# SyncE's queue: the address loads of all sorted blocks ahead of the ninth block's rows, the first finished batch's store five loads later

## The chip, the cores and the metric

One core of one Trainium2 chip. The time is the device time of one execution in microseconds. Three runs of the kernel before gave 222.42, 222.91 and 529.38 us, a median of 222.91 us.

## The reference

Eight sequences of 375 frames with 128 features go through three layers: a convolution bottleneck with feed-forward and a max-pool over three frames, softmax attention inside each sequence, and a mixture of eight experts of which each frame takes its best two. Cut to the expert layer, which the change touches:

```
gate_logits = relu(xf @ gw1 + gb1) @ gw2 + gb2
top_w, top_idx = top_k(softmax(gate_logits), 2);  top_w = softmax(top_w)
combine[t, top_idx] += top_w
for e in range(8):
    out += combine[:, e:e+1] * (gelu(xf @ we1[e] + be1[e]) @ we2[e] + be2[e])
return h + out
```

## The kernel before

Every engine works through a list of pieces that is written out by hand (`PE_ORDER`, `DVE_ORDER`, `ACT_ORDER`, `POOL_ORDER`, `SP_ORDER`); a piece is a name and a number, and it first waits on the semaphores of what it needs. Each list is executed strictly in order, so a piece that waits holds everything behind it on its engine.

The expert layer is done in two ways. Three of the eight sequences (0, 6, 7) are dense: TensorE computes all eight experts for them (`D1` L1182 and `D2` L1189), and VectorE adds each result with its weight (`da`, L930). These pieces are mixed into the whole second half as filler. The other five sequences are sorted: GpSimd scatters each row twice, by expert, into the scratch array `xs` in HBM (`scat`, L541; each expert has 2048 places), and the sorted rows are worked through in blocks of 128.

There are 37 blocks. Blocks 0 to 7 are the first block of each expert; their place in `xs` and their weights (already in SBUF as `w_all`) are known when the kernel is written. Blocks 8 to 36 are the further ones. Which expert each belongs to is known only when all rows are counted: VectorE writes the table `tab_x` (L951) with the first row of each. SyncE reads it one number at a time into a register:

- `rg.n` (L422): load block n's first row from `tab_x` into a register; in the trace a TENSOR_LOAD, a FUSED_REGOPS and a SEQ_ASSERT. `rg.8` to `rg.36`, 29 of them. The register is kept until block n's pieces have used it.
- `lx.n` (L436): fetch the 128 rows of block n from `xs` into one of 18 buffers `blk_x` (64.5 KB). `lx.0` waits until all 30 scatters have landed (s_scat); `lx.n` waits for `T.(n-9)` on TensorE and, from n = 18, for the scatter that used its buffer.
- `lw.n` (L444), n from 8: copy the block's expert's weights from `w_all` into one of seven buffers `blk_w` (321 KB, SBUF to SBUF), at a register offset. From n = 15 it waits for `yv.(n-7)`, the last reader of the buffer's former content.
- `od.n` (L464, L466): store a finished dense sequence; `od.0` waits for the eighth `da`. `c4` (L429) are copies for the scatters, `yl` (L453) loads of the results at the end, `out` stores of the sorted sequences.

On TensorE a block is `T.n` (L1198, transpose of `blk_x`), `L1.n` (L1205, first product) and `L2.n` (L1214, second product). VectorE or ScalarE copies after `T` (`xT`, L817, L666), ScalarE does the gelu (`gl`, L672), VectorE the bias and copy to `yblk` (`yv`, L956), and GpSimd scatters `yblk` into `ys` (`so`, L547). When all of `ys` has landed, SyncE loads it back (`yl`), VectorE combines (`fin`, L965, L971) and SyncE stores. All copies, from whichever queue, run on the core's 16 DMA engines.

A few pieces of `PE_ORDER` around the blocks that are named later: `T.8 T.9 L2.5 ... L1.8` (the first use of a `blk_w`), `... L2.11 T.15 L1.13`, `T.24 D1.32`, `L2.24 T.28`, `D1.35 T.32 T.33 L2.30`.

Of the kernel before, what the change touches and what calls it, by code (L numbers as in the profile page):

```python
# [120 lines left out]
so.27 so.28 so.29 so.30 so.31 so.32 so.33 so.34 so.35 so.36  # L121
"""
SP_ORDER = """
c4.1 c4.2 c4.3 c4.4 c4.5 rg.8 rg.9 rg.10 rg.11 rg.12 rg.13 rg.14 rg.15 od.0 rg.16 rg.17 rg.18 rg.19 rg.20 rg.21
rg.22 rg.23 rg.24 rg.25 rg.26 lx.0 lx.1 lx.2 lx.3 lx.4 lx.5 lx.6 lx.7 lx.8 lw.8 lx.9 lw.9 lx.10 lw.10 lx.11 lw.11
rg.27 lx.12 rg.28 lw.12 lx.13 lw.13 lx.14 lw.14 lx.15 rg.29 rg.30 lw.15 lx.16 lw.16 lx.17 lw.17 lx.18 lw.18 lx.19
lw.19 rg.31 lx.20 lw.20 rg.32 rg.33 lx.21 lw.21 lx.22 lw.22 lx.23 lw.23 lx.24 lw.24 rg.34 lx.25 lw.25 lx.26 lw.26
lx.27 lw.27 lx.28 lw.28 rg.35 lx.29 lw.29 lx.30 lw.30 lx.31 lw.31 lx.32 lw.32 lx.33 lw.33 lx.34 lw.34 rg.36 lx.35
lw.35 lx.36 lw.36 yl.0 yl.1 yl.2 od.1 yl.3 out.0 yl.4 out.1 out.2 out.3 od.2 out.4
"""  # L130


# [1128 lines left out]
```

How the kernel before makes its waits and increments, by code:

```python
        def wait(eng, name, value):  # L333
            if value > 0:
                eng.wait_ge(S[name], value)
# [15 lines left out]
        def wait_so(eng, n):  # L351
            if n >= 0:
                eng.wait_ge(s_so[n % YBUF], 16 * NT * (n // YBUF + 1))
# [4 lines left out]
        def weights(eng, n):  # L359
            if n < E:
                eng.wait_ge(S["be1"], 1)
                return w_all[:, n, :]
            eng.wait_ge(s_bw[(n - E) % WSLOTS], 16 * ((n - E) // WSLOTS + 1))
            return blk_w[(n - E) % WSLOTS][:]
# [17 lines left out]
        @block.sync  # L383
# [24 lines left out]
            for c in range(HC):  # L408
                sp.dma_start(w_all[:, :, H + c * D:H + (c + 1) * D],
                             we2[:, c * 128:(c + 1) * 128, :].rearrange("e p d -> p e d")).then_inc(S["wt"], 16)
            sp.dma_start(w_all[:, :, 2 * H + HC:WROW], be2.unsqueeze(0).broadcast_to([128, E, D])).then_inc(S["wt"], 16)
            sp.dma_start(be2_sb[:], be2).then_inc(S["wt"], 16)
            sp.wait_ge(S["blank"], 2)
            sp.dma_start(xs.rearrange("(q p r) d -> p q (r d)", p=128, r=RI),
                         blank[:].rearrange("p r d -> p (r d)").unsqueeze(1).broadcast_to([128, PER // RI, RI * XW]))\
# [9 lines left out]
                    wait_nth(sp, "xn4", n)  # L425
                    if k >= 2:
                        sp.wait_ge(s_copy[k % 2], 32 * (k // 2))
                    for lo, hi in SPLIT:
# [2 lines left out]
                    i = n % SLOTS  # L431
                    if n == 0:
                        sp.wait_ge(s_scat, 16 * NI * NS)
                    wait(sp, "T", n - LOADS + 1)
```

## Time and profile before

| | |
|---|---|
| Median of three runs | 222.91 us |
| The profiled execution | 221.66 us, its span 219.9 us, mean granted TensorE clock 0.993 |
| Busy in the span | PE 204.4 us (93%), PE weight loads 166.6, DVE 154.4 (70%), ACT 136.9 (62%), POOL 112.9 (51%) |
| Chain that ended last | PE 71%, DVE 8%, SyncE's queue 6%, ACT 5%, issue 4%, DMA 3% |

The span is the profiled part of the execution; the 1.76 us between it and the execution's time lie outside. A share of the chain is the time that the chain of work that ended last spent on that engine. Block numbers do not stand in the trace; they follow from the order lists by counting.

### The profile page before, as it was taken

What the parts mean: (1) busy time and instruction counts of PE and PEld (TensorE: products, weight loads), DVE (VectorE), ACT (ScalarE), POOL (GpSimd) and SP (SyncE); (2) the same over time, 40 slices, a digit from 0 to 9 for tenths busy, and PEclk for the clock granted to TensorE, in tenths of its full rate; (3) what the DMA queues carried; (4) which work ended last, traced back from release to release, by engine and by line L of the source; (5) the groups of instructions that cost most, each with busy time, mean ns of one, the idle gap of its engine ahead of it and who ended that gap; (6) DMA issues with size and microseconds to landing.
All of it is one profiled execution on the core that took longest, in us unless ns stands there. A gap on an engine that the chain in (4) does not pass through costs nothing.

```text
span 219.9 us, 5429 instructions
## 1 busy us (share of the span) xinstructions
PE 204.4 (93%) x1553; PEld 166.6 (76%) x1553; DVE 154.4 (70%) x688; ACT 136.9 (62%) x302; POOL 112.9 (51%) x168
## 2 busy tenths in 40 slices
PE   6997788999999999999999999999999989699990
PEld 5864656659857986898678967889989768599780
DVE  6379999998998998979599944484426233224895
ACT  2234997998989688776679248456655547335430
POOL 7746776611630147676774775015777766472000
PEclk9999999999999999999999999999999999999997
DMA  5999999940010012102111121587597898712773
GB/s 157 244 270 305 330 405 406 402 170 3 0 35 1 3 35 58 53 23 80 52 47 37 38 70 48 141 259 246 165 308 232 286 303 304 270 36 71 195 226 106
DMA packets 26000, 35.31 MB, mean 161 GB/s; under 512 B 4083, under 2 KB 18838, under 8 KB 25971
## 3 DMA queue, kind: packets, MB, share of 16 engines
q1 hardware_dynamic: 23137, 30.60, 43.4%
q0 software_dynamic: 2240, 4.00, 5.8%
q10 hardware_dynamic: 594, 0.36, 0.6%
q8 instruction: 13, 0.21, 0.4%
q14 instruction: 16, 0.13, 0.2%
HBM read 10.61 MB, written 14.39 MB: 114 GB/s over the span
## 4 chain that ended last, share of the span: by engine, by line
PE 71%; DVE 8%; SPq 6%; ACT 5%; issue 4%; DMA 3%; POOL 1%; DVEq 0%; ACTq 0%
PE PS L1189 11%; PE PS L1182 10%; PE PS L1124 7%; PE PS L1106 7%; PE PS L1214 5%; PE PS L1205 4%; PE PS L989 4%; PE PS L1113 4%; DMA blk_x<-xs 3%; PE PS L1001 3%; SPq L444 3%; PE PS L1101 3%; PE PS L1018 2%; SPq L436 2%; DVE acc L965 2%
## 5 line engine op out<-in xcount | busy, mean ns | idle before, releaser
L547 POOL DMA_INDIRECT ys<-yblk,blk_x x37 | 36.0, 973 | 28.1 <-DVE yblk L956 19.3
L517 POOL TENSOR_TENSOR rstd<-mv,mhalf 125x3 f32<-125x3 f32 x32 | 27.7, 867 | 41.0 <-DVE mv L698 40.7
L661 ACT ACTIVATE gd<-PS,bias 128x373 f32<-128x373 f32 x48 | 27.1, 574 | 15.4 <-PE PS L1182 10.8
L541 POOL DMA_INDIRECT xs<-rows_x,pos_x x30 | 29.9, 996 | 13.0 <-issue 8.4
L1182 PE MATMUL PS<-xt_sb,w_all 128*128 128x373 f32 x96 | 35.7, 482 | 0.0
L1189 PEld LDWEIGHTS PS<-w_all,gd 128*125 128x125 f32 x288 | 33.6, 187 | 2.1
L1189 PE MATMUL PS<-w_all,gd 128*125 128x128 f32 x288 | 34.6, 273 | 0.0
L672 ACT ACTIVATE gb_t<-PS,blk_w 128x128 f32<-128x128 f32 x58 | 18.1, 365 | 15.1 <-issue 8.8
L930 DVE SCALAR_TENSOR_TENSOR x_sb<-PS,comb,x_sb 125x128 f32<-125x128 f32 x72 | 20.7, 343 | 5.8 <-PE PS L1189 4.9
L1182 PEld LDWEIGHTS PS<-xt_sb,w_all 128*128 128x128 f32 x96 | 15.7, 190 | 5.0 <-issue 0.9
L956 DVE TENSOR_TENSOR yblk<-PS,blk_w 128x128 f32<-128x128 f32 x29 | 8.4, 290 | 15.8 <-PE PS L1214 15.5
L1106 PE MATMUL PS<-xn_t,q_t 128*125 128x373 f32 x48 | 17.8, 486 | 0.0
L1124 PE MATMUL PS<-xn,prob_t 125*125 125x129 f32 (+1 forms) x144 | 17.6, 275 | 0.0
L1214 PE MATMUL PS<-blk_w,gb_t 128*128 128x128 f32 x116 | 17.4, 277 | 0.0
L1124 PEld LDWEIGHTS PS<-xn,prob_t 125*125 125x125 f32 (+1 forms) x144 | 16.7, 187 | 0.8 <-issue 0.4
L1205 PE MATMUL PS<-xb_t,blk_w 128*128 128x128 f32 x116 | 17.2, 275 | 0.0
L817 DVE COPY xb_t<-PS 128x128 f32<-128x128 f32 x27 | 7.8, 289 | 13.2 <-PE PS L1198 10.6
L1205 PEld LDWEIGHTS PS<-xb_t,blk_w 128*128 128x128 f32 x116 | 15.5, 191 | 1.8 <-issue 0.3
L1214 PEld LDWEIGHTS PS<-blk_w,gb_t 128*128 128x128 f32 x116 | 15.0, 191 | 0.7 <-issue 0.3
L831 DVE TENSOR_REDUCE nmax<-PS 125x1 f32<-125x373 f32 x24 | 12.8, 544 | 2.6 <-PE PS L1106 1.8
L637 ACT ACTIVATE prob_t<-PS 124x373 f32<-124x373 f32 (+1 forms) x23 | 9.9, 482 | 6.0 <-PE PS L1113 5.6
L631 ACT ACTIVATE prob<-PS,nmax 125x373 f32<-125x373 f32 x24 | 12.5, 573 | 1.5 <-DVE nmax L831 1.2
(201 smaller groups left out, 409.4 us busy)
## 6 DMA issues: line engine op xcount, KB each, us to landing
blk_w<-w_all SPq DMA_DIRECT2D x29, 321.0 KB, 3.1
xs<-blank SPq DMA_DIRECT2D x1, 8256.0 KB, 25.3
blk_x<-xs SPq DMA_DIRECT2D x37, 64.5 KB, 3.0
yg<-ys SPq DMA_DIRECT2D x5, 336.0 KB
x_sb<-in_x SPq DMA_DIRECT2D x4, 336.0 KB
out<-x_sb SPq DMA_DIRECT2D x8, 168.0 KB
xt_sb<-in_xt SPq DMA_DIRECT2D x3, 375.0 KB, 5.4
w_all<-in_we SPq DMA_DIRECT2D x1, 1024.0 KB
```

The costliest lines, as they stand in the source:

```text
L517: pool.tensor_tensor(rstd[i][:, n % 2, :], mv[i][:, n % 2, :, 1], mhalf[:], ALU.pow)\
L541: pool.indirect_dma_start(xs, bass.IndirectOffsetOnAxis(ap=pos_x[:, b // 2, s, i:i + 1], axis=0), rows_x[:, k, s, j, :], None, bounds_chec ...
L547: pool.indirect_dma_start(ys, bass.IndirectOffsetOnAxis(ap=blk_x[n % SLOTS][:, t, D:XW].bitcast(u32), axis=0), yblk[n % YBUF][:, t, :], No ...
L661: act.activation(gd[:, k % GD, c, 0:TP], of("D1", n)[:, 0:TP], ACT.Gelu, bias=bias128[:, 2 + k % E * HC + c:3 + k % E * HC + c]).then_inc( ...
L672: last = act.activation(gb_t[n % 2][:, c, :], of("L1", n)[:, c * BLK:(c + 1) * BLK], ACT.Gelu, bias=w[:, 2 * H + c:2 * H + c + 1])
L930: last = dve.scalar_tensor_tensor(flat(h2[:, b, :])[j], flat(of("D2", n)[0:P, :])[j], w[:, j, b % 2, e:e + 1], flat(h2[:, b, :])[j], ALU.m ...
L1106: pe.matmul(f[0:P, 0:TP], q_t[:, s, OFF[j]:OFF[j] + P], xn_t[:, s, :], start=True, stop=True)\
L1124: last = pe.matmul(f[0:P, j * (D + 1):(j + 1) * (D + 1)], prob_t[0:ROWS[c], s, c, OFF[j]:OFF[j] + P], xn3[0:ROWS[c], s, c, :], start=(c == ...
L1182: pe.matmul(f[:, 0:TP], w_all[:, k % E, c * 128:(c + 1) * 128], x32[:, DENSE[k // E], 0:TP], start=True, stop=True).then_inc(S["D1"], 1)
L1189: last = pe.matmul(f[0:P, j * D:(j + 1) * D], gd[:, n % GD, c, OFF[j]:OFF[j] + P], w_all[:, n % E, H + c * D:H + (c + 1) * D], start=(c == ...
L1205: last = pe.matmul(f[:, c * BLK:(c + 1) * BLK], w[:, c * 128:(c + 1) * 128], xb_t[n % 2][:], start=True, stop=True)
L1214: last = pe.matmul(f[:, t * D:(t + 1) * D], gb_t[n % 2][:, c, t * 128:(t + 1) * 128], w[:, H + c * D:H + (c + 1) * D], start=(c == 0), sto ...
```

## The change

Only `SP_ORDER` differs: the same pieces, in another order.

```diff
-c4.1 c4.2 c4.3 c4.4 c4.5 rg.8 rg.9 rg.10 rg.11 rg.12 rg.13 rg.14 rg.15 od.0 rg.16 rg.17 rg.18 rg.19 rg.20 rg.21
-rg.22 rg.23 rg.24 rg.25 rg.26 lx.0 lx.1 lx.2 lx.3 lx.4 lx.5 lx.6 lx.7 lx.8 lw.8 lx.9 lw.9 lx.10 lw.10 lx.11 lw.11
-rg.27 lx.12 rg.28 lw.12 lx.13 lw.13 lx.14 lw.14 lx.15 rg.29 rg.30 lw.15 lx.16 lw.16 lx.17 lw.17 lx.18 lw.18 lx.19
-lw.19 rg.31 lx.20 lw.20 rg.32 rg.33 lx.21 lw.21 lx.22 lw.22 lx.23 lw.23 lx.24 lw.24 rg.34 lx.25 lw.25 lx.26 lw.26
-lx.27 lw.27 lx.28 lw.28 rg.35 lx.29 lw.29 lx.30 lw.30 lx.31 lw.31 lx.32 lw.32 lx.33 lw.33 lx.34 lw.34 rg.36 lx.35
-lw.35 lx.36 lw.36 yl.0 yl.1 yl.2 od.1 yl.3 out.0 yl.4 out.1 out.2 out.3 od.2 out.4
+c4.1 c4.2 c4.3 c4.4 c4.5 rg.8 rg.9 rg.10 rg.11 rg.12 rg.13 rg.14 rg.15 rg.16 rg.17 rg.18 rg.19 rg.20 od.0 rg.21
+rg.22 rg.23 rg.24 rg.25 rg.26 rg.27 rg.28 rg.29 rg.30 rg.31 lx.0 lx.1 lx.2 lx.3 lx.4 lx.5 lx.6 lx.7 rg.32 rg.33
+rg.34 rg.35 rg.36 lx.8 lw.8 lx.9 lw.9 lx.10 lw.10 lx.11 lw.11 lx.12 lw.12 lx.13 lw.13 lx.14 lw.14 lx.15 lw.15
+lx.16 lw.16 lx.17 lw.17 lx.18 lw.18 lx.19 lw.19 lx.20 lw.20 lx.21 lw.21 lx.22 lw.22 lx.23 lw.23 lx.24 lw.24
+lx.25 lw.25 lx.26 lw.26 lx.27 lw.27 lx.28 lw.28 lx.29 lw.29 lx.30 lw.30 lx.31 lw.31 lx.32 lw.32 lx.33 lw.33
+lx.34 lw.34 lx.35 lw.35 lx.36 lw.36 yl.0 yl.1 yl.2 od.1 yl.3 out.0 yl.4 out.1 out.2 out.3 od.2 out.4
```

`od.0` stands behind `rg.20` instead of `rg.15`. `rg.27` to `rg.31` stand ahead of `lx.0`; before, they were spread from `lx.12` to `lx.20`. `rg.32` to `rg.36` stand between `lx.7` and `lx.8`; before, they were spread from `lx.21` to `lx.35`. Behind `lx.8` nothing but `lx` and `lw` is left until `yl.0`.

## Rows read from the trace of the kernel before

**Rows 1.** Busy time by stretch: us from:to, PE PEld DVE ACT POOL, clock, DMA share, GB/s

```profile
156.00:188.90 32.90, 29.70 (x230) 26.43 (x228) 11.55 (x43) 18.59 (x58) 23.35 (x24) 1.00 0.84 281
175.00:180.00 5.00, 4.03 (x29) 3.28 (x28) 1.56 (x6) 2.81 (x8) 3.19 (x5) 1.00 0.94 309
...
170.00:180.00 10.00, 8.53 (x63) 7.33 (x62) 3.12 (x12) 5.34 (x17) 6.96 (x9) 1.00 0.88 293
180.00:190.00 10.00, 8.27 (x63) 7.09 (x62) 2.82 (x11) 5.37 (x16) 5.72 (x6) 1.00 0.88 301
190.00:205.00 15.00, 15.00 (x117) 13.60 (x116) 6.28 (x24) 6.11 (x16) 6.82 (x7) 1.00 0.33 101
205.00:220.00 15.00, 9.30 (x61) 7.50 (x59) 11.89 (x45) 4.01 (x7) 0.00 (x0) 0.89 0.59 169
```

**Rows 2.** TensorE in order of time, L1198: T.15, T.24, T.28, T.33 [idle before]

```profile
158.34 0.27 PE L1198 MATMUL PS<-ident,blk_x 128*128 128x128 f32 x1
...
174.18 0.33 PE L1198 MATMUL PS<-ident,blk_x 128*128 128x128 f32 x1 [0.50 <-DMA blk_x<-xs]
...
179.50 0.33 PE L1198 MATMUL PS<-ident,blk_x 128*128 128x128 f32 x1 [0.84 <-DMA blk_x<-xs]
...
188.90 0.33 PE L1198 MATMUL PS<-ident,blk_x 128*128 128x128 f32 x1 [1.73 <-DMA blk_x<-xs]
```

**Rows 3.** SyncE's queue in order of time: start, us, issue; from lx.0 on

```profile
136.75 4.27 SPq L436 DMA_DIRECT2D blk_x<-xs  x9
...
151.53 0.46 SPq L436 DMA_DIRECT2D blk_x<-xs  x1
156.00 0.51 SPq L444 DMA_DIRECT2D blk_w<-w_all  x1
...
161.46 0.50 SPq L444 DMA_DIRECT2D blk_w<-w_all  x1
162.80 0.35 SPq L436 DMA_DIRECT2D blk_x<-xs  x1
...
167.89 0.50 SPq L444 DMA_DIRECT2D blk_w<-w_all  x1
...
174.40 0.50 SPq L444 DMA_DIRECT2D blk_w<-w_all  x1
175.15 0.40 SPq L436 DMA_DIRECT2D blk_x<-xs  x1
...
177.07 0.49 SPq L444 DMA_DIRECT2D blk_w<-w_all  x1
178.62 0.34 SPq L436 DMA_DIRECT2D blk_x<-xs  x1
...
183.90 0.38 SPq L436 DMA_DIRECT2D blk_x<-xs  x1
```

**Rows 4.** The address loads, L422, of 119 to 128.1 us: min/median/max ns

```profile
L422 SPq TENSOR_LOAD <-tab_x x8: 264/266/487, 120.0 to 124.1; - x8
```

**Rows 5.** SyncE's waits over the span: total us, times, longest

```profile
SPq L464 <- DVE x_sb L930: 3.9, 2, 3.5
SPq L444 <- DVE yblk L956: 2.5, 1, 2.5
...
SPq L436 <- DMA xs<-rows_x,pos_x: 0.6, 1, 0.6
```

**Rows 6.** Block fetches L436, 141 to 191 us: issue to landing

```profile
DMA to landing us min/median/max: 2.6/3.3/4.0
```

**Rows 7.** VectorE in order of time: yv.15

```profile
165.68 0.29 DVE L956 TENSOR_TENSOR yblk<-PS,blk_w 128x128 f32<-128x128 f32 x1 [0.71 <-PE PS L1214]
```

**Rows 8.** GpSimd in order of time: the scatters so.4 and so.36

```profile
153.72 0.98 POOL L547 DMA_INDIRECT ys<-yblk,blk_x  x1 [0.30 <-DVE yblk L956]
...
198.45 0.97 POOL L547 DMA_INDIRECT ys<-yblk,blk_x  x1 [0.30 <-issue]
```

## The prediction

> **What bounds the kernel now.** I read busy time by stretch first, then TensorE in order of time, then SyncE's queue, to see who holds whom. TensorE is the engine to follow: it is busy for all 15.00 us from 190 to 205, and the end behind that is a chain on VectorE (11.89 of 15 us) that starts from TensorE's last dense products [rows 1]. In the sorted stage it is not full: from 156 to 188.9 us it works 29.70 of 32.90 us, so 3.20 us are lost, 1.47 of them from 170 to 180 and 1.73 from 180 to 190 [rows 1]. The reader is to see in rows 2 what ends these gaps: three times the transpose of a block waits for its rows, T.24 for 0.50 us, T.28 for 0.84 and T.33 for 1.73, each released by a DMA into blk_x; the rest of the 1.47 is shorter pieces of the same kind. The trace names no other cause of idle time there.
>
> Why are the rows late? Two suspects. One is SyncE's sequencer: from 156 on it hands out a fetch and a weight copy per block and hardly ever waits; its only long wait on `yv` is the 2.5 us that end at lw.15, 156.00 [rows 3, 5]. A pair without a load between takes about 1.3 us, since the gap from an issued lw to the next lx is 0.25 us (174.90 to 175.15) [rows 3]. Where a load of an address stands in the gap, it is 0.84 us (lw.19 ends at 161.96, lx.20 begins at 162.80) and 1.06 us (177.56 to 178.62) [rows 3]: a load costs SyncE 0.59 to 0.81 us, I take 0.7. The other suspect is the DMA engines: their mean share over the same 32.9 us is 0.84, over 170 to 190 it is 0.88, and the fullest five microseconds have 0.94 [rows 1]. Both are near their limit, and that decides the size of the gain.
>
> **The change part by part.** Ahead of the batch store: five loads (rg.16 to rg.20) move ahead of od.0. Eight loads began at 120.0, the last at 124.1 [rows 4], so one costs here some 0.59 us, and od.0 then waited up to 3.5 us for VectorE [rows 5]. Five loads take 2.9 us (3.5 at 0.7) and fit into this wait. od.0 keeps its time, and its own three issues are not longer. Behind od.0 stood eleven loads, and again eleven stand there (rg.21 to rg.31), so lx.0 keeps its time, 136.75; there it waited 0.6 us for the scatters [rows 5], which is a second cushion. Cost 0; without the cushion in od.0 the five would push lx.0 by 2.9 less 0.6.
>
> Ahead of lx.8: five loads (rg.32 to rg.36) now stand in front of it, uncovered on SyncE. lx.8, the last of the nine fetches that end at 141.02 [rows 3], goes 3.0 to 4.1 us later (5 x 0.59 to 5 x 0.81). Queued behind are lw.8 and all later pairs. By lx.15, today issued at 151.53, two removed loads (rg.27, rg.28) have given time back, so three are left: 1.8 to 2.4 us, issued at 153.3 to 153.9. With 3.3 us to landing (4.0 at most [rows 6]) it lands at 156.6 to 157.9, and T.15 is due at 158.34 [rows 2]: the tightest place of the front, and it holds by 0.4 us at the worst corner. lw.15 then has four removed loads against five added ones, one load late, 0.6 to 0.8 us, inside the 2.5 us that SyncE waited there for yv.8. At 156.00 the old and new queues are therefore level. Cost 0; if the cover is gone, T.14 and T.15 are late next.
>
> Behind 156.00: six loads (rg.31 to rg.36) are gone, 6 x 0.7 = 4.2 us of SyncE. What can take their place is the ring of seven weight buffers: lw.22, today 167.89, may go no sooner than yv.15, which ends at 165.97 [rows 3, 7], so at most 1.9 us sooner where three loads would give 2.1. That limit moves along when TensorE is no longer held, as `yv` follows TensorE. At lx.24 one gets some 1.6 to 2.1 us, more than T.24's 0.50; at lx.28 four loads, 2.8 us, more than the 0.84. So I count the whole 1.47 us of 170 to 180 as won.
>
> T.33 is the place that sets the size. TensorE is ready for it at 188.90 - 1.73 = 187.17 today, and at 185.70 once 1.47 are won. lx.33 has five loads ahead of it: issued at 183.90 - 3.5 = 180.4, and at today's 5.0 us from issue to use (183.90 to 188.90 [rows 2, 3]) it would be there at 185.4, in time. But those 5.0 us, against a median of 3.3 [rows 6], say that this fetch stood in a backlog. By the DMA engines: from 156 to 188.9 they did 0.84 x 32.9 = 27.6 us of full work. At 0.94 this takes 29.4 us and ends at 185.4, at 0.88 it takes 31.4 and ends at 187.4. Between the two ends I take 0.91, as the stream has no gaps left but the share of 0.88 was reached over 20 us that held three of the loads: 30.3 us, 186.3, so T.33 still waits 0.6 us. The gain is 3.20 - 0.6 = 2.6 us; the ends are 0 (share stays 0.84) and 3.20 (all idle time of TensorE).
>
> The Trainium skill ("DMA: Bandwidth & Descriptors", Rules for kernel authors) speaks against the change here: spreading DMAs over issuing engines brings no bandwidth, because all run on the same 16 engines, it only saves the sequencer's issue time. Issue time is also all that this change saves; by that rule alone the gain would be near the low end, by SyncE's rows alone the full 3.2.
>
> Behind the blocks: GpSimd scatters back to back every 1.28 us (0.98 and 0.30 idle). From so.4 at 153.72, 32 of these put so.36 at 194.7, today it is at 198.45 [rows 8], so this queue allows 3.8 us and doesn't stop 2.6. TensorE's full stretch from 190 and VectorE's tail [rows 1] shift as they are; the loads of the results wait for so.36 and shift as well.
>
> **Sum.** 0 + 0 - 2.6 on the profiled execution's 221.66 gives 219.1. The median, 222.91, is 1.25 us above that execution; on its scale it is 220.3. A measurement of this kernel can tell about 2%, 4.5 us, from no change, and the gain is below that.
>
> **The rivals.**
> The DMA engines are the bound. For it: 0.88 over 20 us, the backlog at lx.33. Against: they stood at 0.94 for five microseconds, and each removed load is a gap in the issue stream. At 0.88, T.33 waits until 187.4, 1.7 us, and the gain is 1.5: 221.4. The skill's rule above is this case.
> No gain at all: the new order's 29 addresses held at once (19 in the old) do not fit SyncE's registers and are read again at use, or the waits on TensorE come from latency and just move. For it: the trace shows 19 held, not 29. Against: exactly one TENSOR_LOAD to each of the eight [rows 4], so nothing is reread at 19. 222.9.
> Slower: the front is not covered, because loads in a burst cost more than those seen. At 1.5 us each, lx.0 is late by 5 x 1.5 - 3.5 - 0.6 = 3.4, lx.8 by 10.9, lx.15 (two loads of 0.7 given back) by 9.5; it lands at 151.53 + 9.5 + 3.3 = 164.3, T.15 waits 6.0, less the 3.2 behind: 2.8 slower, 225.7. It decides from 1.2 us a load on (lx.15 late by 6.5, T.15 by 3.0, about even). Against: eight in a row took 0.59 each [rows 4], the dearest here 0.81.
>
> **How the numbers follow.** The forecast 0.58, gain 2.0 to 3.2, its own range 219.7 to 220.9. The DMA engines as the bound 0.20. No gain 0.11. The slower case 0.05. Faster by more than 4.5 us 0.06: only if SyncE's lead brings more than TensorE's idle time, or through scatter of runs. The range is 218.8 to 222.7: down by all 3.20 us and, for scatter, somewhat more than the 0.5 us between the two ordinary runs; up to nearly no change, which leaves out the slower case, half of no gain and the far gains. Slower by over 2% is half of the slower case and a little scatter, 0.03; faster 0.06; within, 0.91.
>
> **What would show it.** Right: od.0 still near 128.1 and lx.0 near 136.75; lx.8 three to four us later; lw.15 still released by yv.8 near 156.0, its wait shorter than 2.5; no address load behind lx.8; lx.33 3 us or more sooner; T.24 and T.28 without a wait and T.33 with under 1 us; the DMA share above 0.88 from 160 to 185; the last `yv` 2.6 us sooner. Wrong: TensorE waits at T.8 to T.15 (front), SyncE waits on `yv` at many lw (the ring of seven took over), or T.33 waits as long as before with fetches of 5 us and more (DMA engines).

## The result and the profile after

The changed kernel took 219.51 us (median of 9 runs, 218.91 to 221.61), the kernel before beside it 222.38 us (9 runs); the ratio is 0.9892, 95% interval 0.9856 to 0.9928, so 2.4 us (1.6 to 3.2) of gain. A repetition gave 218.63 against 222.88 us, ratio 0.984 (0.9791 to 0.9888), 3.6 us. Both are clear of no change. The first is below 2%; the interval of the second reaches 2.1%. A ratio is taken from the single runs and is not the quotient of the two medians, which would give 2.9 and 4.3 us.

The profiled execution is not a typical one but the longest of the nine: 221.61 us, its span 219.9 us, exactly that of the kernel before. Compared by their ends, the two traces would show nothing. Busy time by stretch of the changed kernel (us from:to, PE PEld DVE ACT POOL, clock, DMA share, GB/s), around the place where the two executions part:

```profile
18.00:20.00 2.00, 0.72 (x15) 0.34 (x7) 1.97 (x5) 0.20 (x1) 1.36 (x2) 1.00 1.11 346
20.00:22.00 2.00, 2.00 (x25) 1.29 (x24) 1.66 (x8) 1.01 (x2) 0.75 (x1) 0.50 1.19 292
22.00:24.00 2.00, 2.00 (x12) 0.69 (x8) 1.69 (x10) 1.28 (x3) 1.93 (x3) 0.64 1.20 290
24.00:26.00 2.00, 1.43 (x29) 1.04 (x28) 0.87 (x3) 1.97 (x3) 0.39 (x2) 1.00 1.13 364
```

and the same view of the kernel before:

```profile
18.00:20.00 2.00, 1.10 (x19) 0.91 (x23) 1.93 (x6) 0.80 (x2) 0.76 (x1) 1.00 1.10 341
20.00:24.00 4.00, 3.27 (x52) 1.84 (x45) 3.50 (x17) 3.73 (x6) 3.07 (x5) 1.00 1.18 294
```

From 20 us on the granted clock was at the lower of its two levels, 1.2 GHz (0.50), for most of four microseconds in the one and at 2.4 in the other, long before any instruction that the change moves; in the two microseconds ahead TensorE had worked 0.72 and 1.10 us. The first address load already comes 2.0 us later (at 122.0 instead of 120.0 us), and so does the sorted stage: T.0 at 143.47 instead of 141.44, od.0 at 130.12 instead of 128.11. So the stage is to be measured from its own first transpose. From T.0 to the start of the last `yv` the kernel before takes 55.4 us (141.44 to 196.86), the changed one 53.3 (143.47 to 196.79): 2.1 us of gain, near the 2.4 us of the ratio. What follows the start of the last `yv` takes 23.1 us in both.

TensorE in order of time, L1198, with the only waits for rows that the profile still names:

```profile
175.54 0.27 PE L1198 MATMUL PS<-ident,blk_x 128*128 128x128 f32 x1
...
180.59 0.33 PE L1198 MATMUL PS<-ident,blk_x 128*128 128x128 f32 x1 [0.88 <-DMA blk_x<-xs]
...
187.98 0.38 PE L1198 MATMUL PS<-ident,blk_x 128*128 128x128 f32 x2
...
191.90 0.33 PE L1198 MATMUL PS<-ident,blk_x 128*128 128x128 f32 x1 [0.57 <-DMA blk_x<-xs]
```

These are T.24, T.28, T.32 with T.33, and T.35. Against [rows 2]: T.24's 0.50 and T.33's 1.73 are gone, T.28 kept 0.88 and T.35 has a new 0.57. SyncE's queue, same kernel (start, us, issue):

```profile
130.12 0.85 SPq L464 DMA_DIRECT2D out<-x_sb  x2
...
138.70 7.02 SPq L436 DMA_DIRECT2D blk_x<-xs  x9
...
154.64 0.44 SPq L436 DMA_DIRECT2D blk_x<-xs  x1
158.01 0.50 SPq L444 DMA_DIRECT2D blk_w<-w_all  x1
...
171.13 2.08 SPq L444 DMA_DIRECT2D blk_w<-w_all  x1
...
184.49 0.38 SPq L436 DMA_DIRECT2D blk_x<-xs  x1
```

The nine first fetches now span 7.02 us instead of 4.27 [rows 3]: five loads for 2.75 us, 0.55 each. One issue, lw.24, takes 2.08 us where 0.50 is usual, and lx.25 to lx.28 stand behind it: that T.28 waits here for this reason is borne out by the repetition below, where lw.24 takes 0.49 us and T.28 does not wait. At T.35 something is added: lx.35, still late behind lw.24, was issued at 187.15, and its rows took 4.7 us to land, where those of lx.32 took 2.8. The landing of lx.35:

```profile
DMA to landing us min/median/max: 4.7/4.7/4.7
```

The last row of the queue above is lx.33: 41.0 us behind T.0, in the kernel before 42.5. SyncE's waits at an lw, the longest of them that of lw.15 for yv.8 (total us, times, longest):

```profile
SPq L444 <- DVE yblk L956: 3.7, 3, 2.8
```

It was 2.5 in one wait [rows 5]; the copies in the middle of the stage touch the ring of seven twice more, for 0.9 us together. Busy time by stretch, the rows that answer to [rows 1]:

```profile
156.00:188.90 32.90, 31.98 (x255) 29.30 (x254) 12.63 (x48) 19.53 (x60) 24.33 (x26) 1.00 0.87 289
170.00:180.00 10.00, 9.67 (x77) 8.79 (x75) 4.22 (x17) 5.66 (x18) 7.57 (x8) 1.00 0.83 266
180.00:190.00 10.00, 9.41 (x71) 8.38 (x72) 3.46 (x14) 5.64 (x18) 6.89 (x8) 1.00 0.97 328
```

TensorE loses 0.92 of 32.9 us (3.20 before). These stretches are fixed on the clock and the stage is not, and T.35's wait lies behind them. From T.0 to the last `yv` of each execution (before, changed, changed repeated):

```profile
141.44:196.86 55.42, 52.13 (x404) 47.08 (x404) 23.90 (x86) 29.85 (x94) 34.03 (x35) 1.00 0.73 244
143.47:196.79 53.32, 51.74 (x404) 47.09 (x404) 23.90 (x86) 29.86 (x94) 34.00 (x36) 1.00 0.76 253
143.51:195.04 51.53, 51.45 (x404) 47.06 (x404) 23.80 (x87) 29.93 (x94) 33.99 (x35) 1.00 0.78 262
```

The idle time of TensorE is 3.29, 1.58 and 0.08 us. And the chain that ended last:

```profile
PE 76%; DVE 9%; ACT 4%; DMA 4%; issue 3%; POOL 2%; SPq 1%; DVEq 0%; ACTq 0%
```

SyncE's queue fell from 6% to 1% of it, TensorE rose from 71% to 76%.

### The profile page after: what moved, and what is told of

It reads as the page before. It is cut to its first block, busy times and chain, and to the rows that moved or that the text cites. A ratio compares the mean times of both kernels' runs of the same rounds, so it can differ in the third digit from the quotient of the medians.

```text
span 219.9 us, 5429 instructions
## 1 busy us (share of the span) xinstructions
PE 206.2 (94%) x1553; PEld 167.3 (76%) x1553; DVE 154.4 (70%) x688; ACT 136.8 (62%) x302; POOL 112.7 (51%) x168
## 4 chain that ended last, share of the span: by engine, by line
PE 76%; DVE 9%; ACT 4%; DMA 4%; issue 3%; POOL 2%; SPq 1%; DVEq 0%; ACTq 0%
PE PS L1189 12%; PE PS L1182 11%; PE PS L1124 7%; PE PS L1106 7%; PE PS L1205 6%; PE PS L1214 6%; PE PS L1113 4%; PE PS L989 4%; DMA blk_x<-xs 4%; PE PS L1001 3%; PE PS L1101 3%; DVE acc L965 2%; PE PS L1198 2%; DVE x_sb L930 2%; DVE x_sb L971 2%
## 5 line engine op out<-in xcount | busy, mean ns | idle before, releaser
L956 DVE TENSOR_TENSOR yblk<-PS,blk_w 128x128 f32<-128x128 f32 x29 | 8.4, 290 | 14.6 <-PE PS L1214 14.2
```

## The experiments

In the table, "stage" is the time from the start of the first T to the start of the last `yv` in the profiled execution, and "waits" are TensorE's waits at T that the profile names (a wait of T.0 lies ahead of the stage). Each stage and each wait is read from a single execution. Ratios are against the kernel before on the same chip.

| kernel | median us | before | ratio, 95% | stage us | waits at T, us |
|---|---|---|---|---|---|
| before | | | | 55.4 | 3.1 |
| changed | 219.51 | 222.38 | 0.9892 (0.9856 to 0.9928) | 53.3 | 1.5 |
| changed, repeated | 218.63 | 222.88 | 0.984 (0.9791 to 0.9888) | 51.5 | 0 |
| store back | 220.18 | 223.09 | 0.9894 (0.9855 to 0.9932) | 53.0 | 1.7 |
| rear loads only | 220.17 | 223.09 | 0.9856 (0.9821 to 0.989) | 53.4 | 1.2 |
| front only | 222.73 | 223.09 | 0.9975 (0.9945 to 1.0006) | 55.1 | 2.6 |
| three loads early | 221.45 | 223.09 | 0.9889 (0.9846 to 0.9932) | 54.8 | 2.0 |
| light copies, changed | 219.67 | 222.88 | 0.9896 (0.9845 to 0.9947) | 51.2 | 0 |
| light copies, before | 220.97 | 222.88 | 0.993 (0.99 to 0.9959) | 53.6 | 1.5 |
| rows three ahead, changed | 219.03 | 222.88 | 0.9876 (0.9823 to 0.9928) | 51.4 | 0 |

**Store back.** The changed kernel with the store where it was:

```diff
-... rg.15 rg.16 rg.17 rg.18 rg.19 rg.20 od.0 rg.21 ...
+... rg.15 od.0 rg.16 rg.17 rg.18 rg.19 rg.20 rg.21 ...
```

> The changed kernel with the first batch's store back behind rg.15; all loads stay ahead. Theory S (the gain is only the six address loads taken out of SyncE's stream behind 156 us): the store waits for VectorE up to 3.5 us with nothing to do, then 16 loads instead of 11 follow before lx.0, so lx.0 is 5 x 0.6 - 0.6..1.0 = 2.0 to 2.4 us later against the first transpose than in the changed kernel; T.0 is due about 4.7 us after lx.0 with some 2 us to landing, so T.0 is not held; lx.8 to lx.15 come 2 to 2.4 us later still, and T.14 or T.15 waits 0.5 to 2 us. Time 0 to 2 us above the changed kernel (219.5 to 221.5), still at or below the kernel before. Rival F (the store's place is worth nothing, all slack): the same as the changed kernel within 0.3 us and no wait of TensorE before T.20.

Measured: the ratio of the changed kernel. TensorE in order of time shows what the missing cushion costs at the head, and SyncE's waits what it used up:

```profile
141.99 0.33 PE L1198 MATMUL PS<-ident,blk_x 128*128 128x128 f32 x1 [0.45 <-DMA blk_x<-xs]
```

```profile
SPq L444 <- DVE yblk L956: 0.2, 1, 0.2
```

T.0 waits 0.45 us, lx.0 going out at 138.96 instead of some 136.7 (138.70 less the 2.03), and lw.15 waits 0.2 us for yv.8, where the changed kernel's longest wait at an lw is 2.8. T.0 did wait, against my expectation, and T.14 and T.15, for which I expected 0.5 to 2 us, did not. So the store's move, with five loads in its shadow, is worth under half a microsecond in this profile and nothing that the ratios can tell; what it mainly buys is a reserve. Rival F's "no wait before T.20" is wrong by this 0.45.

**Rear loads only.** The kernel before with the six last loads moved, nothing else:

```diff
-... lx.7 lx.8 lw.8 ... lw.19 rg.31 lx.20 lw.20 rg.32 rg.33 lx.21 ... rg.34 lx.25 ... rg.35 lx.29 ... rg.36 lx.35 ...
+... lx.7 rg.31 rg.32 rg.33 rg.34 rg.35 rg.36 lx.8 lw.8 ... lw.19 lx.20 lw.20 lx.21 ... lx.25 ... lx.29 ... lx.35 ...
```

> The kernel before with only rg.31 to rg.36 moved, to between lx.7 and lx.8; the store and rg.27 to rg.30 stay where they were. Theory S: the whole gain, ratio 0.987 to 0.991 against the kernel before (2.0 to 2.9 us); TensorE's idle time from the first T to the last L2 falls from 3.2 to about 1.2 us; lw.15 still waits for yv.8, by 1 us or so less. Rival D (the DMA engines are the bound and the gain came from the earlier loads and the store): under 1 us.

Measured: ratio 0.9856, stage 53.4 us. The whole gain is here, without the front. TensorE's waits, 130 us to the end:

```profile
PE PS L1198 <- DMA blk_w<-w_all: 0.5, 1, 0.5
PE PS L1198 <- DVE yblk L956: 0.4, 1, 0.4
PE PS L1198 <- DMA blk_x<-xs: 0.3, 1, 0.3
```

L1198 is a T, which reads neither blk_w nor yblk, so the names of the first two releasers can't be taken at their word; their time, 0.9 us, can. In order of time the waits are those of T.19 (0.3 us), T.28 (0.4) and T.35 (0.5). One thing came out otherwise than expected: lw.15 does not wait for yv.8 at all and goes out 15.3 us behind T.0 instead of 14.6. The six loads ahead of lx.8 have used up the whole wait; in the changed kernel, which has the front part too, it is 2.8 us.

**Front only.** The store behind rg.20 and rg.27 to rg.30 ahead of lx.0, the rear loads in their old places:

```diff
-... rg.15 od.0 rg.16 ... rg.26 lx.0 ... lw.11 rg.27 lx.12 rg.28 lw.12 ... lx.15 rg.29 rg.30 lw.15 ...
+... rg.15 rg.16 ... rg.20 od.0 rg.21 ... rg.30 lx.0 ... lw.11 lx.12 lw.12 ... lx.15 lw.15 ...
```

> The kernel before with only the front part of the change: the store behind rg.20 and rg.27 to rg.30 ahead of lx.0; rg.31 to rg.36 stay in the stream. Theory S: no gain, 0 +- 0.4 us against the kernel before, T.24, T.28 and T.33 wait as before (3 us in all), since lw.15 still waits for yv.8 and only waits longer (2.5 us becomes about 4). Rival F: 1 us or more of the gain.

Measured: 0.9975 with 1 inside the interval. SyncE turned what it saved into waiting for yv.8:

```profile
SPq L444 <- DVE yblk L956: 5.0, 1, 5.0
```

2.5 us became 5.0, and TensorE waited 2.6 us at T as before (0.88, 0.51, 1.22). Nine loads moved ahead (five into the store's wait, four ahead of lx.0) buy nothing by themselves.

**Three loads early.** The kernel before with rg.31 to rg.33 between lx.7 and lx.8 and rg.34 to rg.36 in place.

> The kernel before with three of the six rear loads (rg.31, rg.32, rg.33) moved ahead of lx.8; rg.34, rg.35 and rg.36 stay. Theory S: what counts is how far ahead SyncE is at T.24, T.28 and T.33; three loads give 2.1 us there, so T.24's 0.5 and T.28's 0.84 go and T.33's 1.7 shrinks to under 1.2: 1.5 to 2.4 us of gain, over half of the full one. Rival (only the last wait counts, loads near it): half or less, 0.5 to 1.3 us.

Measured: ratio 0.9889, 2.5 us, at the upper end of what theory S expects; but the profiled execution, the longest of the six, is nearer the rival: stage 54.8 us, 0.7 gained, with TensorE's waits

```profile
179.93 0.33 PE L1198 MATMUL PS<-ident,blk_x 128*128 128x128 f32 x1 [0.50 <-DMA blk_x<-xs]
...
189.65 0.33 PE L1198 MATMUL PS<-ident,blk_x 128*128 128x128 f32 x1 [1.54 <-DMA blk_x<-xs]
```

T.24's wait went, T.28 kept 0.50 of 0.84, T.33 1.54 of 1.73. In this execution SyncE took 1.33 us for lx.26 at 173.96, which takes back more than one of the three loads; lx.33 went out 42.1 us behind T.0, only 0.4 sooner than in the kernel before, and its rows took 4.7 us to land. (A second slow issue, 1.22 us at 186.89, is lw.34 and stands behind lx.33.) Whether half the loads bring half the gain or more is not decided.

**Fewer bytes, and rows further ahead, first try.** Four kernels went to a chip on which the kernel before took 249.28 us instead of 222 to 223; in each of their traces there are four to six stretches of 0.4 to 1.4 us, at changing places, in which no engine works at all; the kernel before on its usual chip has none. "Light copies" leaves the number of instructions alone and copies 256 of 642 columns of the weights:

```diff
-sp.dma_start(blk_w[k % WSLOTS][:], w_all[:, bass.ds(row_of_block[n] // CAP, 1), :]...)
+sp.dma_start(blk_w[k % WSLOTS][:, 0:H], w_all[:, bass.ds(row_of_block[n] // CAP, 1), 0:H]...)
```

and "rows three ahead" shifts the fetches against the copies:

```diff
-... lx.15 lw.15 lx.16 lw.16 lx.17 lw.17 ... lx.36 lw.36
+... lx.15 lx.16 lx.17 lx.18 lw.15 lx.19 lw.16 lx.20 lw.17 ... lx.36 lw.33 lw.34 lw.35 lw.36
```

Light copies in the changed kernel:

> The changed kernel with weight copies of 256 of 642 columns (128 KB instead of 321); the second product, the gelu's bias and the bias of the block take fixed weights of w_all instead, so the time is that of the same instructions with 0.4 of the weight bytes. Number of SyncE's instructions unchanged. Theory D (what is left of TensorE's waits is the load of the DMA engines): the DMA share from 156 to 189 falls from 0.87 to under 0.6, the remaining 1.5 us of waits at T are gone, the time falls by 0.7 to 1.5 us against the changed kernel. Rival S2 (what is left is SyncE's pace or single slow issues of 1 to 2 us): waits of 0.5 us and more remain and the time stays within 0.4 us of the changed kernel.

In the kernel before:

> The kernel before with the same lighter weight copies (256 of 642 columns, second product and biases from fixed weights). If SyncE's issue alone set the waits (theory S in its pure form), T.24, T.28 and T.33 still wait, 2 us or more in all, and the time is within 0.7 us of the kernel before. If the backlog of the DMA engines was part of the cause (theory D), the waits fall to under 1 us and the time falls by 2 to 3 us, to that of the changed kernel: either remedy, earlier issue or fewer bytes, would do.

Rows three ahead in the changed kernel:

> The changed kernel with the row fetches three blocks ahead of the weight copies from lx.16 on (lx.16 to lx.18 ahead of lw.15, then lx.n+3 ahead of lw.n): they fill SyncE's wait for yv.8 and every block's rows are issued some 4 us sooner. Theory: all waits on TensorE in the stage are at T, on rows; then they go, 0.8 to 1.5 us below the changed kernel (218.0 to 218.7). Rival: the weight copies are now late by three fetches (1.8 us), L1 waits instead or the ring of seven holds SyncE, and the time is the same or up to 0.5 us longer.

In the kernel before:

> The kernel before, loads left in the stream, with the same lead of three blocks for the row fetches. Theory: rows issued about 4 us sooner cover the 0.5, 0.84 and 1.73 us waits as well as taking the loads out: 2 to 3.2 us below the kernel before, level with the changed kernel. Rival: the loads still delay the weight copies, and L1 waits where T did: under 1 us of gain.

Measured: 0.9934 (0.9883 to 0.9985), 1.0059 (0.9993 to 1.0125), 0.9932 (0.9882 to 0.9981), 1.0024 (0.9982 to 1.0066). The two that build on the changed kernel are ahead of the kernel before, the two that keep the loads in the stream are not. The traces carry no reading of single waits, so three of them were run again on the same chip, when it gave the kernel before 222.88 us, with the changed kernel beside them. Rows three ahead with the loads left in place was not repeated and stays open.

**Changed kernel, repeated.**

> The changed kernel once more, on the chip of the three that follow. Theory S: T.0 to the last yv takes 53.0 to 53.6 us (55.4 in the kernel before), ratio 0.985 to 0.992 against the kernel before; where the granted clock does not fall ahead of the sorted stage, the span is 217.2 to 218.2 us and not 219.9.

Measured: ratio 0.984, stage 51.5 us, a span of 218.1 although the clock fell in this execution too. Busy time by stretch:

```profile
20.00:24.00 4.00, 4.00 (x33) 1.97 (x32) 3.35 (x17) 2.29 (x5) 2.68 (x3) 0.57 1.18 300
```

```profile
156.00:188.90 32.90, 32.90 (x264) 30.33 (x263) 13.42 (x51) 19.89 (x62) 25.06 (x26) 1.00 0.92 310
170.00:180.00 10.00, 10.00 (x83) 9.35 (x82) 4.30 (x17) 5.64 (x19) 7.61 (x8) 1.00 0.96 332
180.00:190.00 10.00, 10.00 (x76) 8.83 (x75) 3.56 (x13) 6.29 (x20) 7.77 (x8) 1.00 0.99 339
```

TensorE has no idle time in the stage and the DMA engines reach 0.99 while every row is in time. From T.0 to lx.33 it is 39.4 us here (143.5 to 182.92), 3.0 less than before: nearly what five loads cost. Between this execution and the first one of the same kernel lies lw.24: 0.49 us at 171.15 here, 2.08 us at 171.13 there. This execution has two slow issues as well, lx.7 with 1.27 us and lw.16 with 1.30, but they stand where there is a reserve: the one ahead of lw.15's wait, which shrank to 1.9 us, the other right behind it.

**Light copies in the changed kernel, second try** (the second product and the biases use fixed weights, so the time is that of the same instructions with fewer bytes).

> The changed kernel with weight copies of 256 of 642 columns (second product and biases from fixed weights of w_all). The earlier run of it was on a chip that held up every engine for microseconds at a time, so this one is for the question itself. Theory D: DMA share from 156 to 189 under 0.6, the 1.5 us of waits at T gone, T.0 to the last yv 51.8 to 52.3 us, 0.7 to 1.5 us below the changed kernel. Rival S2 (single slow issues of 1 to 2 us on SyncE set what is left): T still waits 0.5 us or more and the time is within 0.4 us of the changed kernel.

Measured: DMA share 0.59, no waits, stage 51.2 us; median 219.67 against 218.63 for the changed kernel on this chip, intervals overlapping. Once the loads are gone, 0.4 of the weight bytes is worth at most the 0.4 us of the stage, and nothing in the medians. That the bytes held the 1.5 us of waits of the first profile is not decided by this run, since the repeated execution with all the bytes has no waits either. The end of this kernel is another one, too: behind the start of the last `yv` the span goes on for 24.6 us and not 23.1, because the chain that ends last no longer runs through TensorE's last dense products but through the last scatter and the load of the results. First this kernel, then the repeated one (start, us):

```profile
194.53 4.22 DMA ys<-yblk,blk_x
200.10 4.26 DMA yg<-ys
```

```profile
195.00 2.62 PE PS L1189 x24
198.88 3.96 PE PS L1189 x36
```

Whether its other runs end so too, the one trace does not show.

**Light copies in the kernel before, second try.**

> The kernel before with the same lighter weight copies. Pure theory S (issue alone): T.24, T.28 and T.33 still wait 2 us or more in all, T.0 to the last yv 54.5 us or more. Theory S with D (late issue and a backlog of bytes together): waits fall to under 1 us, 52.0 to 53.2 us, and the time is at or below that of the changed kernel.

Measured: ratio 0.993, stage 53.6 us. Its busy time and its waits:

```profile
156.00:188.90 32.90, 32.08 (x252) 28.97 (x250) 13.02 (x49) 19.51 (x61) 24.28 (x25) 1.00 0.54 162
```

```profile
178.48 0.33 PE L1199 MATMUL PS<-ident,blk_x 128*128 128x128 f32 x1 [0.28 <-DMA blk_x<-xs]
179.69 0.33 PE L1199 MATMUL PS<-ident,blk_x 128*128 128x128 f32 x1 [0.43 <-DMA blk_x<-xs]
...
189.63 0.33 PE L1199 MATMUL PS<-ident,blk_x 128*128 128x128 f32 x1 [0.83 <-DMA blk_x<-xs]
```

This lies between both expectations. At a DMA share of 0.54 rows are still late, although the four fetches whose landing the trace holds took only 1.8 to 1.9 us (the kernel before: 2.6, 3.3 and 4.0): that half of the 3.1 us of waits is SyncE's, address loads and one slow issue (lx.24, 1.23 us) together. The other half went with the bytes. The ratios agree: 1.6 us of gain here, 3.6 for the changed kernel on the same chip. The wait before was late issue plus slow landing.

**Rows three ahead in the changed kernel, second try.**

> The changed kernel with the row fetches three blocks ahead of the weight copies from lx.16 on. All waits that are left stand at T, on rows: with rows issued some 4 us sooner they go, T.0 to the last yv 51.8 to 52.5 us, 0.7 to 1.4 us below the changed kernel. Rival: the weight copies are late by three fetches, L1 waits instead or lw is held by the ring of seven, and the time is the same within 0.4 us.

Measured: stage 51.4 us, no waits, median 219.03: the same as the changed kernel. A slow issue of 1.29 us at 173.57 held nobody up, which fits a longer reserve, but no gain shows in the medians. No version was found that beats the changed kernel.

## Why the prediction was right

Forecast 220.3 us and 2.6 us of gain, range 218.8 to 222.7; measured 219.51 us, and 2.4 us by the ratio (0.9892). The mechanism was right; that the size came out so near is partly luck, as the repetition with its 3.6 us shows, which is above the 3.2 us that I gave as the most. Step by step:

- **What a load costs SyncE**: predicted 0.59 to 0.81 us, 0.7 in the stream, 0.59 in a row. In a row it was 0.55. In the stream, T.0 to lx.33 shrank by 3.0 us for five loads in the repeated execution, 0.6 each; this is rough, as each of the two executions has a slow issue in that stretch (lw.25 with 1.04 us before, lw.16 with 1.30 in the repetition).
- **Ahead of the batch store, cost 0**: right. od.0 and lx.0 kept their places against T.0 (lx.0 4.7 us ahead of it before, 4.8 after). Without the cushion in od.0, lx.0 goes out 2.2 us later, against the 2.3 I had named, and T.0 then waits 0.45 us (store back).
- **Ahead of lx.8, cost 0**: right. lx.8 moved by 2.7 us against T.0, predicted 3.0 to 4.1, and lx.15 by 1.1, predicted 1.8 to 2.4; neither T.15 nor any other early T waited. lw.15 went out 14.5 us behind T.0, in the kernel before 14.6.
- **Behind lw.15**: right as a mechanism, and this is where all of it is: rear loads only 0.9856, front only 0.9975.
- **T.33 and the DMA engines**: the size came out right with the argument partly wrong. I capped the DMA engines at 0.91 to 0.94, the fullest stretch seen, and left T.33 0.6 us of wait. They went to 0.97 and 0.99 over ten microseconds, and T.33 did not wait in either execution. What was left instead, 1.5 us in the first profile, was 0.9 at T.28 behind SyncE's slow lw.24, and 0.6 at T.35, whose rows went out late behind the same issue and took 4.7 us to land: a backlog like the one I feared, two blocks further on. Slow issues I had not priced, although the kernel before has three of 0.90 to 1.04 us, one of them (lw.25) ahead of T.28, so that a part of its 3.1 us of waits was not the loads' doing. The two errors nearly cancelled. My 3.3 us from issue to landing, too, stood on only three fetches whose landing the trace holds (2.6, 3.3, 4.0).
- **The upper end of 3.20 us** was too low for the repeated execution: its stage is 3.9 us shorter, more than TensorE's idle time. Of these, 3.2 us are idle time (3.29 to 0.08) and 0.7 are busy time, 52.13 to 51.45 us for the same 404 matmuls. The ends of matmuls are modelled, and a short delay falls inside such a duration: in the kernel before, the rows of T.25 land at 175.3 and T.25 starts at 175.34 and takes 0.33 us instead of 0.27, with no idle time shown. So the idle time that a profile shows is a lower bound of what a stage can gain.
- **The signs.** lw.15's wait was to become shorter than 2.5 us; it was 2.8 in the first profile and 1.9 in the repeated one. lx.33 was to go out 3 us or more sooner; it was 1.5 and 3.0. T.28 was to have no wait and had 0.88 and none. The DMA share from 160 to 185 was 0.90 and 0.94, as named. The last `yv` came 2.1 and 3.9 us sooner behind T.0, named were 2.6.
- **How small a gain can be told**: I said 2%, 4.5 us. With nine runs a side the interval is 0.8 us to either side, and the 2.4 us are clear of no change.
- **The rivals.** DMA engines as the bound: fell, since they carried 0.99 without a wait; but they are half of the cause of the old waits (light copies, before). The rule of the Trainium skill that I set against the change ("DMA: Bandwidth & Descriptors", Rules for kernel authors) is right in its words, issue time is all that is saved, and here the issue time was worth the full gain. The change spreads no copies over queues, and no run here tries that. Registers: 29 loads in both traces, none repeated. Slower front: loads at 0.55 us, far from the 1.2 us where it would have decided.

## What to carry to other kernels

A sequencer that only hands out copies is a resource with a rate: here 1.3 us for a pair of copies and 0.55 to 0.8 us for a register load, against 1.4 us of the stage per block (51.5 us for 37). Work that depends on nothing late belongs ahead of the last place where that queue waits anyway, and only what is taken out behind that place counts. Two executions of one kernel can differ by more than the change (the nine runs of the changed kernel spread over 2.7 us): compare stages from their own first instruction, and repeat the profile before a single wait is explained.

## What was not expected

- The granted clock fell to 1.2 GHz for most of the four microseconds from 20 us on in three of the ten profiles outside the slow chip (both of the changed kernel, front only). T.0 then came at 143.5, in the kernel before at 141.4. It is not all that moves T.0: in four profiles without the fall (rear loads only, three loads early, light copies before, rows three ahead) it came at 142.6 to 142.9. Up to rg.15 the instructions and their order are the same in all ten, and rg.8 already comes at 119.9 to 122.1 us.
- Single issues on SyncE of 0.9 to 2.1 us instead of 0.4 to 0.5 stand in each of these ten profiles, two to four of them, 27 in all. A packet of an instruction queue (q8) lies beside every one of them. For the longest, lw.24 of the changed kernel at 171.13, it is in flight from 170.98 to 172.83 us. The view of 170.0 to 171.2 us shows it:

```profile
q8 instruction: 1, 0.02, 9.6%
```

The Trainium skill ("Runtime: NRT & Kernel Launch", Instruction fetch mechanics) says that a sequencer fetches its instructions in 16 KiB blocks over a DMA queue of its own, with the cost mostly hidden; 0.02 MB fits one block. What the ten traces show: of the 660 issues of rows and weight copies, 58 run beside such a packet, the 27 of 0.9 us and more are all among them, and none of the other 602 takes longer than 0.76 us. Not every packet brings one: the repeated execution has a packet at 172.7 us beside lw.25, which takes 0.49 us, and of the 40 packets in these stretches 12 have no issue beside them that is longer than 0.68 us. So the fetching of instructions and the slow issues go together, and which of them lands ahead of T.28 differs from one execution to the next. Whose instructions queue q8 carries and how it holds up SyncE stays open.
